# Half-wise waits and another order behind the last tile in a merged attention and mixture stage

## The chip, the cores and the metric

The kernel runs on one core of a Trainium2 chip. The time is the device time of one execution in microseconds (us), as a median of several runs. Its engines are TensorE (PE; its weight loads are shown apart as PEld), VectorE (DVE), ScalarE (ACT), GpSimd (POOL) and SyncE (SP, which here only starts DMAs).

## The reference, cut to what matters

The program is a network of four layers, each an attention block and a feed-forward block. The change lies in one stage of it, which does two things at once: the mixture of experts of the third layer, and the attention of the fourth (`_L3_xattn_ref`). That attention takes, for each of 16 heads, 128 queries against 128 keys, keeps the 32 largest scores of each row, takes the softmax over those and applies it to the values:

```python
def _L3_xattn_ref(query, key, value, Wq, Wk):
    NUM_HEADS = 16
    SCALE = DIM_ATTN ** (-0.5)          # DIM_ATTN = 8
    TOP_K = 32
    q = _split_heads(query @ Wq.T, b, sq)
    k = _split_heads(key @ Wk.T, b, sk)
    v = _split_heads(value, b, sk)
    scores = jnp.einsum('bhqa,bhka->bhqk', q, k) * SCALE
    top_vals = jax.lax.top_k(scores, TOP_K)[0]
    cutoff = top_vals[..., -1:]
    masked = jnp.where(scores >= cutoff, scores, -jnp.inf)
    w = jax.nn.softmax(masked, axis=-1)
    e = jnp.einsum('bhqk,bhka->bhqa', w, v)
    return e.transpose(0, 2, 1, 3).reshape(b, sq, d)
```

The result, times a gate, is added to `x` of shape (32, 128, 128).

## The kernel before

The stage is `l3_attention`. Its unit is a tile: one of the 32 batch elements, 128 rows with 16 heads. All engines run at the same time, and each goes through its own written list of steps, in order: `schedule(eng, steps)` walks a counter c and calls each `(step, behind)` of the list with tile c - behind, if that tile exists. On SP, PE and ACT, middle rounds are a hardware loop of four tiles; on POOL and DVE all are written out. Every step begins with waits on semaphores that other engines count up, so an engine that stands in a wait holds back everything behind it in its list. The mixture's steps (`hide`, `output`, `gelu`, `take_y`, `add_experts` and more) run four tiles ahead, so that the last rounds hold attention alone.

The attention of tile c goes like this:
- PE makes `scores`, ACT copies them to SBUF (`take_scores`, L2637).
- DVE finds in `cutoffs` the 32 largest of each row of each head: four rounds of MAX8 (L2754), which gives the next eight, with three MATCH_REPLACE8 (L2756) between, which strike them out. It goes through heads 0 to 7 first (half 0), then 8 to 15 (half 1). Each instruction counts `found` up, FINDS = 112 for a tile.
- POOL negates the largest of each head in `negate_max` (L2393, tile `nm`) once all 112 are counted.
- ACT takes the exponentials of score + nm in `exps` (L2625, 16 instructions, four for each part n of four heads), which wait for `nm`.
- POOL compares the scores with the 32nd largest (`above`, L2409, four instructions for a part) and multiplies the exponentials with that (L2414), in `mask`, part by part. There is one tile `above`, and each comparison waits for the multiplication before it.
- PE transposes the masked probabilities of a part (`turn_probs`, L2511), ACT copies them (`take_p`, L2606, tile `pT`), PE multiplies them with the values (`apply`, L2521). The four parts follow each other.
- DVE divides by the sums (`divide`, L2763 and L2765, tile `o_norm`), POOL adds that to `x` (`add_attention`, L2420).

`exps` and `mask` of a tile run one round behind its `cutoffs`, the transposes, copies and `apply` two rounds behind, `divide` and `add_attention` three. In the round c = 32, the first behind the last `cutoffs` of tile 31, the lists therefore hold: for ACT, the exponentials of tile 31 and then the copies of tile 30; for POOL, `nm` and the masks of tile 31 and the addition of tile 29; for DVE, the division of tile 29.

There is one `o_norm` and one bank for the outputs of `apply`. Hence these two waits, which the diff does not touch:

```python
                def apply(q, c, n):
                    if n == 0:
                        wait(pe, o_ready, q, 1, c)      # divide(c-1) is done
                def divide(q, c):
                    wait(dve, av_mm, q, NQ, NQ * (c + 1))
                    wait(dve, x_done, q, 1, c)          # add_attention(c-1) is done
```

Of the kernel before, what the change touches and what calls it, by code (L numbers as in the profile page):

```python
# [15 lines left out]
NB = 32  # L16
# [2217 lines left out]
def l3_attention(nc, k):  # L2234
# [4 lines left out]
    H, DA, ROUNDS = 16, 8, 4  # L2239
    Q4, NQ = 4, 4  # L2240
    SC = DA ** -0.5
    BODY = 4
    LAST_LAG = 3
    AHEAD = 4
    FIRST = BODY
    LOOPS = (NB - AHEAD - FIRST) // BODY
# [6 lines left out]
    with ExitStack() as ctx:  # L2253
# [10 lines left out]
        top = [s.sb(f"top{i}", [P, ROUNDS, H, 8]) for i in two]  # L2264
        nm = [s.sb(f"nm{i}", [P, H]) for i in two]
# [24 lines left out]
        p, rest, eq = (spare(score[3], i * NE, NB, E) for i in range(3))  # L2290
# [25 lines left out]
        FINDS = (2 * ROUNDS - 1) * H  # L2316
        BASE_STEPS, NORM_STEPS = 3, 10

        def wait(eng, sem, q, per_element, value):

            n = q * int(BODY * per_element) + value
            if not isinstance(q, int) or n >= 1:
                eng.wait_ge(sem, n)

        def schedule(eng, steps, loops=LOOPS, first=-AHEAD):

            def run(q, c):
                for step, behind in steps:
                    if not isinstance(q, int) or 0 <= q * BODY + c - behind < NB:
                        step(q, c - behind)  # L2330

            for c in range(first, FIRST):
                run(0, c)
            if loops:
                with eng.Fori(0, loops) as q:
                    for c in range(FIRST, FIRST + BODY):
                        run(q, c)
            for c in range(FIRST, NB + LAST_LAG - loops * BODY):
                run(loops, c)
# [13 lines left out]
        def in_group(step, at):  # L2353

            return lambda q, u: step(q, u // GT) if u % GT == at else None
# [4 lines left out]
        def for_part(step, n):  # L2360

            return lambda q, c: step(q, c, n)

        with nc.Block() as block:
# [17 lines left out]
            def _(pool):  # L2382
# [4 lines left out]
                    pool.memset(t[:, :, :], 1.0).then_inc(filled, 1)  # L2387
                pool.wait_ge(filled, 4)

                def negate_max(q, c):  # L2390
                    wait(pool, found, q, FINDS, FINDS * (c + 1))
                    wait(pool, probs_done, q, H, H * (c - 1))
                    pool.tensor_scalar(nm[c % 2][:, :], top[c % 2][:, 0, :, 0:1].rearrange("p h o -> p (h o)"), -1.0,  # L2393
                                       None, ALU.mult).then_inc(nm_ready, 1)

                def take_v(q, c):
# [2 lines left out]
                    pool.tensor_scalar(v[c % 4][:, :, 0:DA], v_raw[c % 2][:, :].rearrange("p (h d) -> p h d", h=H),  # L2399
                                       k.tg[:, 3:4], None, ALU.mult).then_inc(v_ready, 1)  # L2400

                def mask(q, c):
                    for n in range(NQ):
                        hs = slice(Q4 * n, Q4 * n + Q4)
                        wait(pool, found, q, FINDS, FINDS * (c + 1))
                        wait(pool, masked, q, NQ, NQ * c + n)
                        for i in range(Q4):
                            h = Q4 * n + i
                            ins = pool.tensor_scalar(above[:, i, :], score[c % 4][:, h, :],  # L2409
                                                     top[c % 2][:, ROUNDS - 1, h, 7:8], None, ALU.is_ge)  # L2410
                        ins.then_inc(compared, 1)
                        wait(pool, compared, q, NQ, NQ * c + n + 1)
                        wait(pool, probs_done, q, H, H * c + Q4 * n + Q4)
                        pool.tensor_tensor(probs[c % 2][:, hs, :], probs[c % 2][:, hs, :], above[:, :, :], ALU.mult  # L2414
                                           ).then_inc(masked, 1)
# [39 lines left out]
                def norm_scale(q, g):  # L2455
                    n = NORM_STEPS * g

                    def done(i):
# [19 lines left out]
                    pool.tensor_tensor(rstd[:, :], spread[:, :], k.neg_half[:, 0:GT], ALU.pow).then_inc(norm_step, 1)  # L2478
                    done(9)
                    pool.tensor_tensor(shift[:, :], mean[:, :], rstd[:, :], ALU.mult).then_inc(norm_step, 1)  # L2480
                schedule(pool, [(negate_max, 1), (in_group(norm_scale, 1), 2 - AHEAD), (take_v, -1), (mask, 1),
                                (add_experts, 1 - AHEAD), (in_group(add_base, 1), -AHEAD),
                                (in_group(stage_weights, 0), -AHEAD), (add_attention, 3)], loops=0)

            @block.tensor
            def _(pe):
# [106 lines left out]
            def _(act):  # L2593
# [24 lines left out]
                    ins.then_inc(y_ready, 1)  # L2618

                def exps(q, c, n):  # L2620
                    if n == 0:
                        wait(act, nm_ready, q, 1, c + 1)
                        wait(act, p_mm, q, NQ, NQ * (c - 1))
                    for h in range(Q4 * n, Q4 * n + Q4):
                        ins = act.activation(probs[c % 2][:, h, :], score[c % 4][:, h, :], ACT.Exp,  # L2625
                                             bias=nm[c % 2][:, h:h + 1]).then_inc(probs_done, 1)
# [44 lines left out]
                for u in two:  # L2671
                    for at in range(2 * EX):
# [11 lines left out]
                               (take_queries, -1), (for_part(gelu, 4), -AHEAD), (for_part(gelu, 5), -AHEAD),  # L2684
                               (for_part(take_p, 2), 2), (for_part(take_scores, 0), -1), (for_part(gelu, 6), -AHEAD),
                               (for_part(gelu, 7), -AHEAD), (in_group(take_bias, 1), -AHEAD),
                               (for_part(take_p, 3), 2), (in_group(take_weights, 0), -AHEAD), (for_part(take_scores, 2), -1)], first=2 - AHEAD)

            @block.vector
            def _(dve):  # L2690
# [49 lines left out]
                def cutoffs(q, c, half):  # L2740
                    t = top[c % 2]
                    n = FINDS // 2 * half
                    first = H // 2 * half
                    if half == 0:
                        wait(dve, masked, q, NQ, NQ * (c - 1))
                        wait(dve, nm_ready, q, 1, c - 1)
                    wait(dve, s_ready, q, NQ, NQ * c + first // Q4 + 2)
                    for step in range(2 * ROUNDS - 1):
                        for h in range(first, first + H // 2):
# [437 lines left out]
```

## Time and profile before

| what | value |
|---|---|
| median of 3 runs | 3108.95 us (3099.05 to 3109.38) |
| the profiled execution | 3108.43 us, its span 3106.5 us |
| DVE's first MAX8 of the stage, its last | 1819.1 us, 2638.2 us |
| the stage's last addition to x | 2671.41 us |
| first work of the stage behind it | 2672.22 us |
| busy over the span | PE 92%, PEld 73%, DVE 65%, ACT 59%, POOL 46% |

Times in the trace count from the span's start. An engine's row says when it started, for how long it ran, and in brackets how long the engine stood idle ahead of it and whose instruction ended that. Several instructions of a kind in a row are merged (x16), and their time is that of all together. PEclk is the clock that TensorE was granted, 1.00 for 2.4 GHz and 0.50 for 1.2 GHz.

### The profile page before, as it was taken

Reading aid. Unit: us, or ns where it says so; the run is one execution under the profiler, and the core shown is the slowest. Engines: PE = TensorE matmul, PEld = TensorE weight load, DVE = VectorE, ACT = ScalarE, POOL = GpSimd, SP = SyncE. Lnnn points to the kernel's source line nnn. Section 1 sums busy time; section 2 is a strip of 40 time slices with the busy share of each in tenths; the row PEclk is TensorE's granted clock in tenths of the full one; section 3 lists DMA queues with packets and bytes.
Section 4 is the critical chain, followed back from the end, with each engine's and each line's share of the span. In section 5 each row is a group of like instructions: output and inputs, shape, how many; then the busy total and the mean of one; then the engine's idle time right before and its main releaser. Section 6 shows DMA issues by size and latency. Waiting matters only on the chain. (4 is left out here: it accounts for less than half of the span.)

```text
span 3106.5 us, 70161 instructions
## 1 busy us (share of the span) xinstructions
PE 2845.7 (92%) x21784; PEld 2260.2 (73%) x21784; DVE 2029.1 (65%) x7986; ACT 1824.0 (59%) x5314; POOL 1430.8 (46%) x1723
## 2 busy tenths in 40 slices
PE   7999969987997989999999899999999995597999
PEld 5888854434775778888888777888888874486676
DVE  4544536764653456666666459999999999486433
ACT  5777734443553356666666567888888873353333
POOL 2122117762542434444444248888887876552000
PEclk9999979987998999999999998999999985597999
DMA  3000023433763311111111000000000000001000
GB/s 114 6 5 6 5 64 74 82 82 112 262 233 94 126 49 54 54 54 54 54 54 54 16 11 13 14 13 13 13 13 13 13 14 32 2 18 36 7 10 11
DMA packets 99460, 151.82 MB, mean 49 GB/s; under 512 B 11312, under 2 KB 39488, under 8 KB 98752
## 3 DMA queue, kind: packets, MB, share of 16 engines
q1 hardware_dynamic: 99296, 149.96, 16.1%
q8 instruction: 63, 1.03, 0.1%
q14 instruction: 101, 0.83, 0.1%
HBM read 103.33 MB, written 46.47 MB: 48 GB/s over the span
## 5 line engine op out<-in xcount | busy, mean ns | idle before, releaser
L1899 POOL TENSOR_TENSOR l2a_probs<-l2a_probs,l2a_inv 128x1024 f32<-128x1024 f32 x128 | 242.5, 1895 | 369.3 <-DVE l2a_inv L2065 369.2
L2010 ACT ACTIVATE l2a_probs<-l2a_s_ps,l2a_nm 128x256 f32<-128x256 f32 x512 | 236.8, 474 | 199.1 <-DVE l2a_nm L2041 199.1
L2754 DVE MAX8 l3a_top<-l3a_work 128x8 f32<-128x128 f32 x1536 | 327.4, 347 | 0.0
L2540 PEld LDWEIGHTS l3a_l2o_ps<-net_arena 128*128 128x128 f32 x2016 | 278.7, 224 | 40.4 <-issue 36.9
L2409 POOL TENSOR_SCALAR l3a_above<-l3a_score,l3a_top 128x128 f32<-128x128 f32 x512 | 300.1, 603 | 16.4 <-POOL l3a_probs L2414 7.7
L2540 PE MATMUL l3a_l2o_ps<-net_arena 128*128 128x128 f32 x2016 | 285.2, 309 | 11.5 <-ACT net_l1f_gate L2616 11.5
L2756 DVE MATCH_REPLACE8 l3a_work<-l3a_top,l3a_work 128x128 f32<-128x128 f32 x1024 | 277.6, 346 | 0.0
L2528 PE MATMUL l3a_l2h_ps<-net_cols,net_arena 128*128 (+1 forms) x1024 | 251.1, 388 | 11.2 <-ACT net_arena L2647 9.2
L2528 PEld LDWEIGHTS l3a_l2h_ps<-net_cols,net_arena 128*128 128x128 f32 x1024 | 185.0, 191 | 64.0 <-ACT net_arena L2647 22.7
L721 ACT ACTIVATE l0a_probs<-l0a_score_ps,l0a_nm 128x128 f32<-128x128 f32 x512 | 180.2, 382 | 73.4 <-DVE l0a_nm L770 73.4
L2647 ACT ACTIVATE net_arena<-l3a_l2h_ps,net_l2f_b 128x256 f32<-128x256 f32 x512 | 210.5, 493 | 16.3 <-PE l3a_l2h_ps L2528 13.7
L2521 PEld LDWEIGHTS l3a_o_ps<-l3a_v,l3a_pT 128*128 128x128 f32 x1024 | 147.8, 216 | 76.7 <-ACT l3a_pT L2606 67.2
L755 POOL TENSOR_TENSOR l0a_v<-l0a_v,l0a_inv 128x1024 f32<-128x1024 f32 x32 | 60.9, 1903 | 300.5 <-DVE l0a_inv L794 300.5
L2521 PE MATMUL l3a_o_ps<-l3a_v,l3a_pT 128*128 128x9 f32 x1024 | 147.5, 272 | 52.7 <-ACT l3a_pT L2606 52.7
L2041 DVE TENSOR_REDUCE l2a_nm<-l2a_s_ps 128x2 f32<-128x512 f32 x256 | 159.0, 684 | 28.3 <-PE l2a_s_ps L1922 28.2
L2414 POOL TENSOR_TENSOR l3a_probs<-l3a_probs,l3a_above 128x512 f32<-128x512 f32 x128 | 163.0, 1274 | 31.3 <-ACT l3a_probs L2625 21.7
L2625 ACT ACTIVATE l3a_probs<-l3a_score,l3a_nm 128x128 f32<-128x128 f32 x512 | 156.8, 398 | 23.1 <-POOL l3a_nm L2393 22.8
L770 DVE TENSOR_REDUCE l0a_nm<-l0a_score_ps 128x4 f32<-128x512 f32 x128 | 82.2, 684 | 124.8 <-PE l0a_score_ps L681 124.8
L2224 DVE SCALAR_TENSOR_TENSOR net_x<-l3f_o_ps,net_weight,net_x 128x128 f32 (+1 forms) x256 | 72.1, 345 | 139.9 <-PE l3f_o_ps L2141 139.5
L2176 ACT ACTIVATE l3f_hidden<-l3f_h_ps 128x512 f32<-128x512 f32 x128 | 76.4, 598 | 145.6 <-PE l3f_h_ps L2132 145.5
L1973 PE MATMUL l2a_side_ps<-net_ident,l2a_probs 128*128 128x128 f32 x1024 | 153.4, 279 | 1.0 <-POOL l2a_probs L1899 0.7
L2756 DVE MATCH_VALUE_LOAD l3a_work<-l3a_top,l3a_work 128x8 f32 x1024 | 150.3, 150 | 0.0
(520 smaller groups left out, 7268.8 us busy)
## 6 DMA issues: line engine op xcount, KB each, us to landing
kv_ahead<-l1a_kept SPq DMA_DIRECT2D x128, 256.0 KB, 2.6
l0f_code<-code_rows SPq DMA_DIRECT2D x32, 512.0 KB, 10.7
l2a_kT<-kv_ahead SPq DMA_DIRECT2D x64, 256.0 KB, 2.6
l2a_v<-kv_ahead SPq DMA_DIRECT2D x64, 256.0 KB, 2.6
l1a_shift<-neg_top SPq DMA_DIRECT2D x16, 512.0 KB, 4.8
l1f_chosen<-mask_code SPq DMA_DIRECT2D x64, 128.0 KB, 3.2
keys_ahead<-l1f_keys_kept SPq DMA_DIRECT2D x32, 256.0 KB, 3.2
l3a_kT<-keys_ahead SPq DMA_DIRECT2D x32, 256.0 KB, 2.6
```

The costliest lines, as they stand in the source:

```text
L721: act.activation(probs[c % 2][:, h, :], score[g][:, i * P:(i + 1) * P], ACT.Exp, bias=nm[:, h:h + 1], accum_out=sums[c % 2][:, h:h + 1]).t ...
L1899: pool.tensor_tensor(p[:, :, :], p[:, :, :], per_row(inv[c % 2][a][:, :, :].rearrange("p i o -> p (i o)"), KV), ALU.mult).then_inc(scaled, 1)
L2010: act.activation(probs[c % 2][a][:, 2 * i + odd, :], s_ps[a][odd][:, i * KV:(i + 1) * KV], ACT.Exp, bias=nm[c % 2][a][:, i, odd:odd + 1], ...
L2041: dve.tensor_reduce(nm[c % 2][a][:, :, odd:odd + 1].rearrange("p i o -> p (i o)"), s_ps[a][odd][:, :].rearrange("p (i s) -> p i s", i=2), ...
L2409: ins = pool.tensor_scalar(above[:, i, :], score[c % 4][:, h, :], top[c % 2][:, ROUNDS - 1, h, 7:8], None, ALU.is_ge)
L2414: pool.tensor_tensor(probs[c % 2][:, hs, :], probs[c % 2][:, hs, :], above[:, :, :], ALU.mult).then_inc(masked, 1)
L2521: ins = pe.matmul(o_ps[:, h, :], pT[n % 2][:, i, :], v[c % 4][:, h, :], start=True, stop=True)
L2528: ins = pe.matmul(h_ps[i][:, n * WIDE:(n + 1) * WIDE], w1[:, expert(u, x), 2 * i + n, :], k.cols[:, ds(group(q, u) * WIDE, WIDE)], start=T ...
L2540: ins = pe.matmul(output_bank(u, x)[:, at:at + D], hidden[2 * x + n][:, i, j * P:(j + 1) * P], w2[:, expert(u, 2 * x + n), i, :], start=(i ...
L2647: ins = act.activation(hidden[x][:, 2 * i + n, :], h_ps[i][:, n * WIDE:(n + 1) * WIDE], ACT.Gelu, bias=b1[:, e, 2 * i + n:2 * i + n + 1])
L2754: ins = dve.max(t[:, step // 2, h, :], src)
L2756: ins = dve.match_replace(work[:, h, :], t[:, step // 2, h, :], src, LOWEST)
```

## The change

It has two parts. First, `negate_max` and `mask` on POOL are split in halves of eight heads: half 0 waits for the first 56 of the 112 finds alone. `exps` waits for the first half of `nm` ahead of part 0, and for the second ahead of part 2. In the running stage both halves of `negate_max` stand one behind the other, and so do both of `mask`.

Second, `schedule` takes another list, `draining`, for the rounds c = 32 and up. On POOL it interleaves the halves: `nm`, mask, `nm`, mask. On ACT it puts the four copies of the tile two back ahead of the sixteen exponentials of the tile one back.

```diff
-        def schedule(eng, steps, loops=LOOPS, first=-AHEAD):
+        def schedule(eng, steps, loops=LOOPS, first=-AHEAD, draining=None):
 
             def run(q, c):
-                for step, behind in steps:
+                drain = draining and isinstance(q, int) and q * BODY + c >= NB
+                for step, behind in draining if drain else steps:
...
-                def negate_max(q, c):
-                    wait(pool, found, q, FINDS, FINDS * (c + 1))
+                def negate_max(q, c, half):
+                    hs = slice(H // 2 * half, H // 2 * (half + 1))
+                    wait(pool, found, q, FINDS, FINDS * c + FINDS // 2 * (half + 1))
                     wait(pool, probs_done, q, H, H * (c - 1))
-                    pool.tensor_scalar(nm[c % 2][:, :], top[c % 2][:, 0, :, 0:1].rearrange("p h o -> p (h o)"), -1.0,
+                    pool.tensor_scalar(nm[c % 2][:, hs], top[c % 2][:, 0, hs, 0:1].rearrange("p h o -> p (h o)"), -1.0,
                                        None, ALU.mult).then_inc(nm_ready, 1)
...
-                def mask(q, c):
-                    for n in range(NQ):
+                def mask(q, c, half):
+                    for n in range(NQ // 2 * half, NQ // 2 * (half + 1)):
                         hs = slice(Q4 * n, Q4 * n + Q4)
-                        wait(pool, found, q, FINDS, FINDS * (c + 1))
+                        wait(pool, found, q, FINDS, FINDS * c + FINDS // 2 * (half + 1))
...
-                schedule(pool, [(negate_max, 1), (in_group(norm_scale, 1), 2 - AHEAD), (take_v, -1), (mask, 1),
+                schedule(pool, [(for_part(negate_max, 0), 1), (for_part(negate_max, 1), 1), (in_group(norm_scale, 1), 2 - AHEAD),
+                                (take_v, -1), (for_part(mask, 0), 1), (for_part(mask, 1), 1),
                                 (add_experts, 1 - AHEAD), (in_group(add_base, 1), -AHEAD),
-                                (in_group(stage_weights, 0), -AHEAD), (add_attention, 3)], loops=0)
+                                (in_group(stage_weights, 0), -AHEAD), (add_attention, 3)], loops=0,
+                         draining=[(for_part(negate_max, 0), 1), (for_part(mask, 0), 1), (for_part(negate_max, 1), 1),
+                                   (for_part(mask, 1), 1), (add_attention, 3)])
...
                 def exps(q, c, n):
+                    if n % 2 == 0:
+                        wait(act, nm_ready, q, 2, 2 * c + n // 2 + 1)
                     if n == 0:
-                        wait(act, nm_ready, q, 1, c + 1)
                         wait(act, p_mm, q, NQ, NQ * (c - 1))
...
+                         draining=[*((for_part(take_p, n), 2) for n in range(NQ)), *((for_part(exps, n), 1) for n in range(NQ))])
...
-                        wait(dve, nm_ready, q, 1, c - 1)
+                        wait(dve, nm_ready, q, 2, 2 * (c - 1))
```

How the instructions stand on ACT behind the last scores, before: the exponentials of tile 30 (x16), the copies of tile 29 (x4), the exponentials of tile 31 (x16), then the copies of tiles 30 and 31 (x8).

```order
L2637 ACTIVATE l3a_score<-l3a_s_ps 128x512 x2
L2625 ACTIVATE l3a_probs<-l3a_score,l3a_nm 128x128 x16
L2606 ACTIVATE l3a_pT<-l3a_p_ps 128x512 x4
L2625 ACTIVATE l3a_probs<-l3a_score,l3a_nm 128x128 x16
L2606 ACTIVATE l3a_pT<-l3a_p_ps 128x512 x8
```

And with the change (its line numbers are some lines higher):

```order
L2643 ACTIVATE l3a_score<-l3a_s_ps 128x512 x2
L2631 ACTIVATE l3a_probs<-l3a_score,l3a_nm 128x128 x16
L2611 ACTIVATE l3a_pT<-l3a_p_ps 128x512 x8
L2631 ACTIVATE l3a_probs<-l3a_score,l3a_nm 128x128 x16
L2611 ACTIVATE l3a_pT<-l3a_p_ps 128x512 x4
```

The four copies of tile 30 moved from behind the exponentials of tile 31 to ahead of them.

On POOL, in the same place, with buffer numbers (tile 31 has `nm1`, `probs1`, `score3`), before:

```order
L2420 TENSOR_TENSOR net_x<-net_x,l3a_o_norm 128x128
L2393 TENSOR_SCALAR l3a_nm1<-l3a_top1 128x16
L2409 TENSOR_SCALAR l3a_above<-l3a_score3,l3a_top1 128x128 x4
L2414 TENSOR_TENSOR l3a_probs1<-l3a_probs1,l3a_above 128x512
L2409 TENSOR_SCALAR l3a_above<-l3a_score3,l3a_top1 128x128 x4
L2414 TENSOR_TENSOR l3a_probs1<-l3a_probs1,l3a_above 128x512
L2409 TENSOR_SCALAR l3a_above<-l3a_score3,l3a_top1 128x128 x4
L2414 TENSOR_TENSOR l3a_probs1<-l3a_probs1,l3a_above 128x512
L2409 TENSOR_SCALAR l3a_above<-l3a_score3,l3a_top1 128x128 x4
L2414 TENSOR_TENSOR l3a_probs1<-l3a_probs1,l3a_above 128x512
L2420 TENSOR_TENSOR net_x<-net_x,l3a_o_norm 128x128 x3
```

With the change:

```order
L2422 TENSOR_TENSOR net_x<-net_x,l3a_o_norm 128x128
L2395 TENSOR_SCALAR l3a_nm1<-l3a_top1 128x8
L2411 TENSOR_SCALAR l3a_above<-l3a_score3,l3a_top1 128x128 x4
L2416 TENSOR_TENSOR l3a_probs1<-l3a_probs1,l3a_above 128x512
L2411 TENSOR_SCALAR l3a_above<-l3a_score3,l3a_top1 128x128 x4
L2416 TENSOR_TENSOR l3a_probs1<-l3a_probs1,l3a_above 128x512
L2395 TENSOR_SCALAR l3a_nm1<-l3a_top1 128x8
L2411 TENSOR_SCALAR l3a_above<-l3a_score3,l3a_top1 128x128 x4
L2416 TENSOR_TENSOR l3a_probs1<-l3a_probs1,l3a_above 128x512
L2411 TENSOR_SCALAR l3a_above<-l3a_score3,l3a_top1 128x128 x4
L2416 TENSOR_TENSOR l3a_probs1<-l3a_probs1,l3a_above 128x512
L2422 TENSOR_TENSOR net_x<-net_x,l3a_o_norm 128x128 x3
```

The second half of `nm` moved behind the second multiplication; the additions of tiles 29, 30 and 31 (x3) still stand last. In every earlier round the one `nm` of 16 columns became two of 8, directly behind each other. PE, DVE and SP have the same instructions in the same order.

## Rows read from the trace of the kernel before

**Rows 1.** The busy time by stretches; columns: stretch, its us, busy us of each engine, PEclk, DMA share, GB/s.
```profile
2400.00:2500.00 100.00, 96.23 (x620) 83.03 (x618) 99.86 (x637) 82.26 (x210) 81.11 (x133) 0.93 0.05 14
...
2640.00:2680.00 40.00, 21.62 (x92) 18.71 (x92) 8.71 (x47) 8.42 (x21) 18.04 (x24) 0.50 0.00 1
```

**Rows 2.** What DVE waited for, 1815 to 2640: us in total, times, longest.
```profile
DVE l3a_top L2754 <- ACT l3a_score L2637: 18.2, 1, 18.2
DVE l3a_inv L2763 <- PE l3a_o_ps L2521: 2.1, 3, 0.9
```

**Rows 3.** What POOL and ACT waited for, 1850 to 2600, the two waits around nm.
```profile
POOL l3a_nm L2393 <- DVE l3a_top L2754: 72.6, 27, 6.4
...
ACT l3a_probs L2625 <- POOL l3a_nm L2393: 6.2, 2, 5.2
```

**Rows 4.** Timeline, 2600 to 2631: start, us, engine, line, what, idle before.
```profile
2600.59 1.69 DVE L2754 MAX8 l3a_top<-l3a_score 128x8 f32<-128x128 f32 x8
...
2603.97 0.45 POOL L2420 TENSOR_TENSOR net_x<-net_x,l3a_o_norm 128x128 f32<-128x128 f32 x1
...
2609.28 1.09 ACT L2637 ACTIVATE l3a_score<-l3a_s_ps 128x512 f32<-128x512 f32 x2 [4.02 <-PE l3a_s_ps L2504]
...
2613.27 0.27 POOL L2393 TENSOR_SCALAR l3a_nm<-l3a_top 128x16 f32<-128x16 f32 x1 [8.85 <-DVE l3a_top L2754]
...
2613.58 1.63 DVE L2754 MAX8 l3a_top<-l3a_score 128x8 f32<-128x128 f32 x8
2613.58 4.80 ACT L2625 ACTIVATE l3a_probs<-l3a_score,l3a_nm 128x128 f32<-128x128 f32 x16 [3.21 <-POOL l3a_nm L2393]
...
2630.95 0.90 PEld L2511 LDWEIGHTS l3a_p_ps<-net_ident,l3a_probs 128*128 128x128 f32 x4
```

**Rows 5.** Timeline, 2636 to 2659, the drain.
```profile
2636.82 1.74 DVE L2754 MAX8 l3a_top<-l3a_work 128x8 f32<-128x128 f32 x8
2638.36 0.35 DVE L2763 RECIPROCAL l3a_inv<-l3a_o_ps 128x16 f32<-128x16 f32 x1
2638.65 0.27 POOL L2393 TENSOR_SCALAR l3a_nm<-l3a_top 128x16 f32<-128x16 f32 x1 [9.42 <-DVE l3a_top L2754]
2638.75 0.29 DVE L2765 TENSOR_TENSOR l3a_o_norm<-l3a_o_ps,l3a_inv 128x128 f32<-128x128 f32 x1
2638.89 2.35 POOL L2409 TENSOR_SCALAR l3a_above<-l3a_score,l3a_top 128x128 f32<-128x128 f32 x4
2638.96 4.80 ACT L2625 ACTIVATE l3a_probs<-l3a_score,l3a_nm 128x128 f32<-128x128 f32 x16 [9.57 <-POOL l3a_nm L2393]
2641.32 1.27 POOL L2414 TENSOR_TENSOR l3a_probs<-l3a_probs,l3a_above 128x512 f32<-128x512 f32 x1
...
2644.29 1.78 PEld L2521 LDWEIGHTS l3a_o_ps<-l3a_v,l3a_pT 128*128 128x128 f32 x8 [12.44 <-ACT l3a_pT L2606]
...
2645.81 0.90 PEld L2511 LDWEIGHTS l3a_p_ps<-net_ident,l3a_probs 128*128 128x128 f32 x4
...
2647.15 0.60 ACT L2606 ACTIVATE l3a_pT<-l3a_p_ps 128x512 f32<-128x512 f32 x1 [2.91 <-PE l3a_p_ps L2511]
2647.80 1.78 PEld L2521 LDWEIGHTS l3a_o_ps<-l3a_v,l3a_pT 128*128 128x128 f32 x8 [1.09 <-ACT l3a_pT L2606]
...
2654.14 0.45 POOL L2420 TENSOR_TENSOR net_x<-net_x,l3a_o_norm 128x128 f32<-128x128 f32 x1
...
2656.72 0.26 DVE L2763 RECIPROCAL l3a_inv<-l3a_o_ps 128x16 f32<-128x16 f32 x1 [17.69 <-PE l3a_o_ps L2521]
2657.02 0.29 DVE L2765 TENSOR_TENSOR l3a_o_norm<-l3a_o_ps,l3a_inv 128x128 f32<-128x128 f32 x1
...
2658.32 1.78 PEld L2521 LDWEIGHTS l3a_o_ps<-l3a_v,l3a_pT 128*128 128x128 f32 x8 [1.09 <-ACT l3a_pT L2606]
```

**Rows 6.** Instructions that use nm, 2500 to 2700: ns min/median/max.
```profile
L2625 ACT ACTIVATE l3a_probs<-l3a_score,l3a_nm x96: 386/389/417, 2513.7 to 2643.4; 128x128 f32<-128x128 f32 x96
```

More of the change, by code:

```diff
@@ L2686, in _ @@
                                (for_part(gelu, 7), -AHEAD), (in_group(take_bias, 1), -AHEAD),
-                               (for_part(take_p, 3), 2), (in_group(take_weights, 0), -AHEAD), (for_part(take_scores, 2), -1)], first=2 - AHEAD)
+                               (for_part(take_p, 3), 2), (in_group(take_weights, 0), -AHEAD), (for_part(take_scores, 2), -1)], first=2 - AHEAD,
+                         draining=[*((for_part(take_p, n), 2) for n in range(NQ)), *((for_part(exps, n), 1) for n in range(NQ))])
             @block.vector
```

## The prediction, made before the changed kernel was run

> **What bounds the kernel now.** Four views, in this order. First the busy time by stretches [rows 1]: from 2400 to 2500 us, a stretch inside the merged stage, DVE is busy 99.86 us of 100, PE 96.23, ACT 82.26, POOL 81.11. Behind the last tile (2640 to 2680) no engine is busy for more than 22 of 40 us and PEclk is 0.50, which is the 1.2 GHz level. Second, what DVE waits for over the whole stage [rows 2]: 18.2 us once, for the first scores, and 2.1 us in three waits of `divide`. So DVE, with `cutoffs`, sets the pace of 32 tiles of some 25.5 us, and nothing that only makes POOL or ACT start earlier can shorten it by more than about 2 us. Third, what POOL and ACT wait for in the running stage [rows 3]: POOL stands 72.6 us in 27 waits, 2.7 us each, ahead of `negate_max`; ACT waits for `nm` in only two of its visits, 6.2 us. ACT usually comes to `exps` after `nm` is ready, so an earlier `nm` buys it nothing there. Fourth, the timeline of the last two tiles [rows 4, 5]: this is where time can move, since from DVE's last MAX8 on everything is one serial chain.
>
> Tiles are 0 to 31; (31,2) means part 2, heads 8 to 11, of tile 31.
>
> **The running stage: 0.** Removed: nothing. Added: one `negate_max` instruction per tile, 0.27 us at most [rows 4], on POOL. It runs while POOL waits for the second half of the maxima anyway (2.7 us on average [rows 3]). Queued behind the second `negate_max` are `take_v` and `mask`, whose wait is for the same find as before. ACT's new wait ahead of `exps` part 2 is for an instruction that ends when the single one did. DVE asks POOL only for the masks of the tile two back: those of tile 29 were done when POOL took the next step at 2603.97, and DVE began tile 31 at 2613.58 [rows 4], 9.6 us of cover. Bounds: -2.1 us if all waits of `divide` vanish [rows 2], +31 x 0.27 = +8.4 us if the cover were gone. I take 0, as 9.6 us of cover is far from gone.
>
> **Tile 30: ACT gains 2.35 us.** At 2609.28 + 1.09 = 2610.37 ACT is free and now stands until 2613.58, for `nm` of tile 30 [rows 4]. POOL is free at 2603.97 + 0.45 = 2604.42, and the first half's maxima are known by then: DVE began the second half of tile 30 at 2600.59. So the first 8 exponentials go into the gap. One costs (4.80 - 0.39) / 15 = 0.294 us in a row [rows 4, 6], so the rest ends 8 x 0.294 = 2.35 us earlier; it can't be more, since the second 8 still wait for DVE's last MAX8. The copies and multiplications of tile 29 shift with it, and the transposes of (30,0) start at 2630.95 - 2.35 = 2628.60.
>
> **Tile 30's copies are ahead of tile 31's exponentials now.** Before, ACT stood in `exps(31,0)` until 2638.96, and `take_p(30,0)` came only behind it, with PE's `apply(30,0)` at 2644.29 [rows 5]. After, `take_p(30,0)` can run at about 2630. But `apply(30,0)` waits for `o_ready` 30, that is for `divide(29)`, and DVE does that behind all cutoffs of tile 31: o_norm is written at 2638.75 to 2639.04 [rows 5]. So the copies stand again, behind a wait that the change leaves in place:
> - `apply(30,0)`: 2639.04 + 0.05 (the hand-off from 2647.15 + 0.60 to 2647.80) = 2639.09, 5.20 earlier than before.
> - From it to the next copy 2647.15 - 2644.29 = 2.86; from part to part 2647.80 - 2644.29 = 3.51. `take_p(30,3)`: 2639.09 + 2.86 + 2 x 3.51 = 2648.97, ending 2649.57.
> - Only then does ACT begin `exps(31,0)`, which before began at 2638.96: 10.6 later. Four exponentials are done after 3 x 0.294 + 0.39 = 1.27: 2650.84.
>
> **POOL's masks of tile 31 are held by that.** POOL has done its half of `nm` and `above` for (31,0) by about 2632; its multiplication stands for `exps(31,0)` until 2650.89, against 2641.32 before: +9.57. Queued behind it on POOL: the rest of mask half 0, the second half of `nm` (done before only if POOL were free; it is not, so it comes at about 2656, though its maxima are there at 2638.4), mask half 1 and `add_attention(29)`. From the first multiplication to that addition took 2654.14 - 2641.32 = 12.82; the inserted `nm` costs 0.24 (2638.65 to 2638.89) but fills the 0.2 us in which POOL waited between two parts, net +0.03. `exps(31,2)` behind the second `nm` takes 1.27 and is ready before its multiplication. `add_attention(29)`: 2650.89 + 12.85 = 2663.74.
>
> **Who waits for the addition.** `divide(30)` needs o_norm free (`x_done` 30), so `add_attention(29)`; `apply(31,0)` needs `divide(30)`. Before, both came in time: the reciprocal at 2656.72 followed PE. After: 2663.74 + 0.45 + 0.05 = 2664.24 reciprocal, + 0.30 + 0.29 for o_norm, + 0.05: `apply(31,0)` at 2664.88 against 2658.32 [rows 5]: **+6.56 us**. The copy (31,0) is ready by about 2659 and doesn't set it. The rest, four parts of 3.51 us and the last division, is the same and moves as a whole, and so does all that follows the stage.
>
> **Sum.** 0 + 6.56. The profiled execution took 3108.43 (span 3106.5), so 3115.0; it is 0.5 under the median of 3108.95, so the median comes to 3115.5. Ten hand-offs of 0.05 to 0.1 us and the early parts add about +-1.5 us.
>
> **A rule that speaks against the change.** DVE's eight MAX8 took 1.63 us while POOL ran `above` beside them (2613.58) and 1.74 us with POOL idle (2636.82) [rows 4, 5], so POOL's company costs DVE nothing here. The change puts `above` of (31,0), 2.35 us, beside the cutoffs of tile 31. The Trainium skill, "SBUF — State Buffer", section "SBUF: two separate sides", says that GpSimd and a VectorE instruction with two SBUF inputs or in a 2-port mode exclude one another for the whole instruction. If that held here, DVE's end and so `apply(30,0)` would be 2.35 us later.
>
> **Rivals.**
> - *The copies run free* (the wait for `divide(29)` doesn't bind). Then the copies of tile 30 follow the transposes at 2628.60 by 1.34 (2645.81 to 2647.15) and end at 2628.60 + 1.34 + 3 x 3.51 + 0.60 = 2641.07; multiplication at 2642.39, addition 2655.24, `apply(31,0)` 1.14 later, 2656.38: -1.9 us, 3107.0. It is what one expects who counts ACT's order alone. The code's wait speaks against it. Chance 0.06.
> - *PE's clock rises in the drain.* At 2.4 GHz PE's share of a 3.51 us part, 2.91, would halve at best, so up to 1.45 us less for each of 3 parts ahead of and 4 behind POOL's chain: -10.2, 3105.3. Against it: PEclk is 0.50 from 2640 to 2680, and 0.93 in the running stage [rows 1], and the change puts a longer pause of PE into it. "TensorE: Matmul & The Clock Gate" in the Trainium skill ("What's actually happening") says that activity releases the throttle. Chance 0.05.
> - *DVE is blocked by POOL's earlier `above`*: 3115.5 + 2.35 = 3117.8, chance 0.03.
> - *Slower by over 0.5%: the stage's pace breaks.* If POOL's masks became the last to release DVE, each of 31 tiles would pay the added instruction, 0.27 + 0.05: +9.9, with the drain +16.5: 3125.4. It decides once POOL ends mask c-2 later than DVE ends tile c-1, that is once 9.6 us of cover are used up. Chance 0.03.
> - *The drain order isn't what the text says*, or a wait is misread: no change, 3109. Chance 0.05.
>
> **How the numbers follow.** Forecast 0.78. A measurement of this kernel can tell about 0.5% (15.5 us) from no change; from 2638.4 to the end of the drain (2658.32 and four parts of 3.51) are some 34 us, and no case moves half of it downward. Of three runs before, one was 10 us lower (3099.05); if the median falls on such a run the forecast reads 3105.5. The range of 3105 to 3119 holds the forecast with this, the two rivals at 3107.0 and 3105.3, no change and the blocked DVE; left out are the broken pace and combinations. Faster 0.02, same 0.94, slower 0.04.
>
> **What would show it.** Right: DVE's last MAX8 unmoved; ACT's last four `take_p` of tile 30 with some 12 us from the first to the second, ended by PE; `exps(31,0)` at about 2649.5; POOL idle from about 2632 to 2651 for ACT; `nm` (31, second half) near 2656; the last but one reciprocal released by POOL's addition, not by PE; the last one, and all behind it, about 6.5 us later. Wrong: copies of tile 30 3.5 us apart throughout (the first rival), weight loads of 0.19 us in the drain (the second), or DVE waits between 1850 and 2600 us.

## The result, and the profile after

The changed kernel takes 3116.12 us (median of 9 runs, 3105.55 to 3119.70), the kernel before 3103.91 us beside it (9 runs, 3099.05 to 3109.38): ratio 1.0026, 95% interval 1.0016 to 1.0036, that is +8.1 us (+5.0 to +11.2); the plain difference of the two medians is 12.2. So it is slower: the interval leaves out 1, though the difference is smaller than the 0.5% (15.5 us) that the prediction took as the least that can be told from no change. The profiled execution took 3113.95 us (span 3112.2), against 3108.43 (span 3106.5) before.

The running stage looks as before. Here are the busy times by stretches, in the columns of [rows 1], of which it answers the first two, and what DVE waited for over the stage, which answers [rows 2]:

```profile
2400.00:2500.00 100.00, 96.31 (x620) 83.16 (x620) 99.86 (x640) 82.19 (x210) 81.79 (x138) 0.93 0.05 14
2620.00:2640.00 20.00, 9.30 (x42) 8.12 (x42) 17.97 (x114) 1.79 (x3) 10.14 (x16) 0.50 0.00 1
2640.00:2680.00 40.00, 19.87 (x84) 16.90 (x84) 3.27 (x16) 8.83 (x23) 13.55 (x20) 0.50 0.00 1
```

```profile
DVE l3a_top L2761 <- ACT l3a_score L2643: 18.2, 1, 18.2
DVE l3a_inv L2770 <- PE l3a_o_ps L2526: 5.1, 3, 2.9
```

From 2400 to 2500 us DVE is again busy 99.86 of 100 us, and POOL's share rose by 0.7 us (81.11 to 81.79). The added instructions cost about that: four tiles pass in this stretch, each with two `nm` of 0.24 us in place of one of 0.27. DVE's three waits for PE are 5.1 us now against 2.1.

The drain is where the two traces part. The timeline of after from the last tile's maxima to the last addition, to be laid beside [rows 5] (columns: start, us, engine, line, what, idle before it and who ended it):

```profile
2627.51 0.90 PEld L2516 LDWEIGHTS l3a_p_ps<-net_ident,l3a_probs 128*128 128x128 f32 x4
...
2628.32 2.33 POOL L2411 TENSOR_SCALAR l3a_above<-l3a_score,l3a_top 128x128 f32<-128x128 f32 x4
...
2628.62 1.64 DVE L2761 MAX8 l3a_top<-l3a_work 128x8 f32<-128x128 f32 x8
2628.86 0.60 ACT L2611 ACTIVATE l3a_pT<-l3a_p_ps 128x512 f32<-128x512 f32 x1 [2.91 <-PE l3a_p_ps L2516]
...
2635.88 1.64 DVE L2761 MAX8 l3a_top<-l3a_work 128x8 f32<-128x128 f32 x8
...
2638.15 1.84 PE L2526 MATMUL l3a_o_ps<-l3a_v,l3a_pT 128*128 128x9 f32 x8 [9.33 <-DVE l3a_o_norm L2772]
...
2640.97 0.60 ACT L2611 ACTIVATE l3a_pT<-l3a_p_ps 128x512 f32<-128x512 f32 x1 [11.52 <-PE l3a_p_ps L2516]
...
2647.99 0.60 ACT L2611 ACTIVATE l3a_pT<-l3a_p_ps 128x512 f32<-128x512 f32 x1 [2.91 <-PE l3a_p_ps L2516]
2648.48 2.43 ACT L2631 ACTIVATE l3a_probs<-l3a_score,l3a_nm 128x128 f32<-128x128 f32 x8
...
2649.89 1.26 POOL L2416 TENSOR_TENSOR l3a_probs<-l3a_probs,l3a_above 128x512 f32<-128x512 f32 x1 [19.25 <-ACT l3a_probs L2631]
...
2654.97 0.24 POOL L2395 TENSOR_SCALAR l3a_nm<-l3a_top 128x8 f32<-128x8 f32 x1
...
2655.25 2.44 ACT L2631 ACTIVATE l3a_probs<-l3a_score,l3a_nm 128x128 f32<-128x128 f32 x8 [4.34 <-POOL l3a_nm L2395]
2657.60 0.57 ACT L2611 ACTIVATE l3a_pT<-l3a_p_ps 128x512 f32<-128x512 f32 x1
...
2662.68 0.45 POOL L2422 TENSOR_TENSOR net_x<-net_x,l3a_o_norm 128x128 f32<-128x128 f32 x1
2663.23 0.26 DVE L2770 RECIPROCAL l3a_inv<-l3a_o_ps 128x16 f32<-128x16 f32 x1 [25.23 <-POOL net_x L2422]
...
2663.93 1.78 PEld L2526 LDWEIGHTS l3a_o_ps<-l3a_v,l3a_pT 128*128 128x128 f32 x8 [12.01 <-issue]
...
2677.03 0.45 POOL L2422 TENSOR_TENSOR net_x<-net_x,l3a_o_norm 128x128 f32<-128x128 f32 x1 [12.68 <-DVE l3a_o_norm L2772]
```

Read it downward as one chain. DVE's last MAX8 comes at 2635.88. PE starts `apply(30,0)` at 2638.15, released by o_norm, that is by `divide(29)`. ACT's copy (30,0) had been done since 2629.46, so the next copy stands 11.52 us for PE. Behind the fourth copy (2647.99) ACT begins the exponentials of tile 31, at 2648.48; POOL has stood 19.25 us for them. POOL's addition of tile 29 begins at 2662.68, and DVE's reciprocal for tile 30 (2663.23) was released by that addition, where in [rows 5] it was PE that released it.

To split the difference I cut each execution at three instructions: the first MAX8 of the stage, the start of its last eight MAX8, and the start of the last addition to x. S is from the first to the second (the running stage), D from the second to the third (the drain). What follows is 434.2 to 435.4 us in all nine kernels. Each S and D is read from the one profiled execution of its kernel.

| | first MAX8 | S | D | rest | span |
|---|---|---|---|---|---|
| before | 1819.1 | 817.7 | 34.59 | 435.1 | 3106.5 |
| after | 1815.4 | 820.5 | 41.15 | 435.2 | 3112.2 |
| difference | -3.7 | +2.8 | +6.56 | +0.1 | +5.7 |

What the change does to the drain is +6.56. The first MAX8 comes between 1813.0 and 1820.4 us in the nine profiles, though none of the edits touches what lies ahead of it, so -3.7 is within what executions differ by. S needs the experiments.

### The profile page after: what moved, and what is told of

It reads as the page before. It is cut to its first block and busy times, and to the rows that moved or that the text cites. A ratio compares the mean times of both kernels' runs of the same rounds, so it can differ in the third digit from the quotient of the medians.

```text
span 3112.2 us, 70259 instructions
## 1 busy us (share of the span) xinstructions
PE 2850.5 (92%) x21784; PEld 2260.4 (73%) x21784; DVE 2027.4 (65%) x7986; ACT 1820.0 (58%) x5314; POOL 1434.3 (46%) x1755
## 5 line engine op out<-in xcount | busy, mean ns | idle before, releaser
L2761 DVE MAX8 l3a_top<-l3a_work 128x8 f32<-128x128 f32 x1536 | 314.1, 276 | 0.0
L2763 DVE MATCH_REPLACE8 l3a_work<-l3a_top,l3a_work 128x128 f32<-128x128 f32 x1024 | 268.9, 275 | 0.0
L2141 PEld LDWEIGHTS l3f_o_ps<-net_arena,l3f_hidden 128*128 128x128 f32 x1024 | 124.2, 192 | 29.7 <-issue 18.2
```

What stands on the lines that cost most here:

```text
L2141: ins = pe.matmul(o_ps[u % OB][:, j * D:(j + 1) * D], hidden[u % 2][:, i, j * P:(j + 1) * P], w2[:, u % E, i, :], start=(i == 0), stop=(i ...
L2761: ins = dve.max(t[:, step // 2, h, :], src)
L2763: ins = dve.match_replace(work[:, h, :], t[:, step // 2, h, :], src, LOWEST)
```

## Experiments: one half of the change at a time

**The halves alone.** The changed kernel without its drain lists, so that ACT and POOL keep the running order behind the last tile:

```diff
-                                (in_group(stage_weights, 0), -AHEAD), (add_attention, 3)], loops=0,
-                         draining=[(for_part(negate_max, 0), 1), (for_part(mask, 0), 1), (for_part(negate_max, 1), 1),
-                                   (for_part(mask, 1), 1), (add_attention, 3)])
+                                (in_group(stage_weights, 0), -AHEAD), (add_attention, 3)], loops=0)
...
-                         draining=[*((for_part(take_p, n), 2) for n in range(NQ)), *((for_part(exps, n), 1) for n in range(NQ))])
```

> The change's first part alone: the waits by halves of eight heads; no other order behind the last tile. Two measures are read from the trace: S, from the stage's first MAX8 to the start of its last eight (817.7 us before, 820.5 with the whole change), and D, from there to the start of the last addition to x (34.6 before, 41.15 with the whole change). My theory (the order of ACT's list costs the drain, the halves gain 2.35 us of exponentials there, the running stage is untouched): D 32.2, S 817.7 +-1, the time 2.4 us under before. Rival A (the halves slow the running stage): S about 820.5, so the time is within 1 us of before. Rival B (the second half of nm, taken late, is what costs the drain): D 34.6 or less as well, since here POOL takes both halves of nm one behind the other; this run doesn't speak against B, the next does.

Measured: 0.9992 of before (0.9981 to 1.0003), S 818.05, D 32.09. The drain is 2.50 us shorter than before. The timeline, in the columns above, shows from where:

```profile
2631.05 1.64 DVE L2758 MAX8 l3a_top<-l3a_work 128x8 f32<-128x128 f32 x8
...
2633.04 2.44 ACT L2629 ACTIVATE l3a_probs<-l3a_score,l3a_nm 128x128 f32<-128x128 f32 x8 [7.08 <-POOL l3a_nm L2395]
2635.39 0.57 ACT L2609 ACTIVATE l3a_pT<-l3a_p_ps 128x512 f32<-128x512 f32 x1
...
2636.01 1.78 PEld L2524 LDWEIGHTS l3a_o_ps<-l3a_v,l3a_pT 128*128 128x128 f32 x8 [12.44 <-ACT l3a_pT L2609]
...
2663.14 0.45 POOL L2422 TENSOR_TENSOR net_x<-net_x,l3a_o_norm 128x128 f32<-128x128 f32 x1 [13.29 <-DVE l3a_o_norm L2769]
```

ACT does only eight exponentials (2.44 us) behind the last maxima, the other eight of tile 31 being done already, and copy (30,0) follows at 2635.39. `apply(30,0)` starts 4.96 us behind the start of the last MAX8 (2636.01 less 2631.05), where it was 7.47 in [rows 5] (2644.29 less 2636.82). So the halves by themselves help the drain, by about the term of 2.35 us that the prediction had given to tile 30 alone. The time alone would not show it: its interval holds 1. S is 818.05, like before: the halves do not slow the running stage. In this run, too, the reciprocal of tile 30 (2648.74) was released by POOL's addition (2648.18), and yet nothing was lost by it: `apply(31,0)` at 2650.05 followed its copy, some 0.7 us after the division would have let it start. A reciprocal that waits for the addition is a loss only where `apply` then waits for the division.

**The new order on ACT alone.** The kernel before, with whole tiles of maxima and exponentials, and only ACT's drain list (with the lines of `schedule` that read it, shown in the change above):

```diff
-                               (for_part(take_p, 3), 2), (in_group(take_weights, 0), -AHEAD), (for_part(take_scores, 2), -1)], first=2 - AHEAD)
+                               (for_part(take_p, 3), 2), (in_group(take_weights, 0), -AHEAD), (for_part(take_scores, 2), -1)], first=2 - AHEAD,
+                         draining=[*((for_part(take_p, n), 2) for n in range(NQ)), *((for_part(exps, n), 1) for n in range(NQ))])
```

> The kernel before with one edit: behind the last tile ACT copies the probabilities of tile 30 ahead of the exponentials of tile 31. No halves, POOL as before. My theory: exps(31,0) begins only behind take_p(30,3), which hangs on divide(29): D 41.1 (+6.5), S 817.7 +-1, the time 6.5 us above before. Rival B (the halves and POOL's late second nm make the drain long): D 34.6, or shorter. Rival A: S 817.7 here, since the halves are not in.

Measured: 1.0015 (1.0004 to 1.0025), S 820.4, D 41.17.

```profile
2637.86 1.64 DVE L2756 MAX8 l3a_top<-l3a_work 128x8 f32<-128x128 f32 x8
...
2642.95 0.60 ACT L2607 ACTIVATE l3a_pT<-l3a_p_ps 128x512 f32<-128x512 f32 x1 [9.15 <-PE l3a_p_ps L2512]
...
2650.46 4.77 ACT L2626 ACTIVATE l3a_probs<-l3a_score,l3a_nm 128x128 f32<-128x128 f32 x16
...
2651.87 1.27 POOL L2415 TENSOR_TENSOR l3a_probs<-l3a_probs,l3a_above 128x512 f32<-128x512 f32 x1 [9.69 <-ACT l3a_probs L2626]
...
2679.03 0.45 POOL L2421 TENSOR_TENSOR net_x<-net_x,l3a_o_norm 128x128 f32<-128x128 f32 x1 [12.68 <-DVE l3a_o_norm L2767]
```

The pattern of after is all there without a single half: a copy that waited 9.15 us for PE, the exponentials behind the fourth copy, POOL idle 9.69 us for them, D within 0.02 us of after's. So the order on ACT makes the loss, and it swallows what the halves win. And S is 820.4 in a kernel whose running stage is that of before, word for word, and where 817.7 +-1 had been expected; its DVE waits ahead of `divide` are 4.8 us. The longer S of after is therefore no effect of the halves. Over all nine profiled executions S is 820.4 to 820.8 where those waits sum to 4.8 to 5.3 us (after, this one, the third experiment), and 817.7 to 818.7 where they sum to 2.1 to 2.9 us (the rest; in the sixth and seventh a wait in the drain is left out, and the three kernels with the early `divide(29)` have its 0.5 us in S). What makes an execution the one or the other stays open.

## Experiments: which wait makes the loss

**The addition ahead of the masks.** The changed kernel; POOL does `add_attention(29)` before it turns to tile 31's masks, so that `divide(30)` has its buffer early:

```diff
-         draining=[(for_part(negate_max, 0), 1), (for_part(mask, 0), 1), (for_part(negate_max, 1), 1),
-                   (for_part(mask, 1), 1), (add_attention, 3)])
+         draining=[(for_part(negate_max, 0), 1), (add_attention, 3), (for_part(mask, 0), 1),
+                   (for_part(negate_max, 1), 1), (for_part(mask, 1), 1)])
```

> The changed kernel with one step moved on POOL behind the last tile: add_attention(29) ahead of the first half of the masks of tile 31, instead of behind the second. D is, as before, the time from the start of the stage's last eight MAX8 to the start of its last addition (34.6 before, 41.15 with the change). My theory: with the change apply(31,0) waits for divide(30), which waits for that addition; moved ahead, the wait is gone and what is late next is the copy (31,0) behind exps(31,3): apply(31,0) 5.7 us earlier than in the change, D 35.5. Rival C: that addition isn't what holds apply(31,0), but the copies or the masks themselves: D 41.

Measured: 0.9995 (0.9981 to 1.0008), D 35.45, 5.70 less than after's.

```profile
2643.14 0.45 POOL L2422 TENSOR_TENSOR net_x<-net_x,l3a_o_norm 128x128 f32<-128x128 f32 x1 [9.76 <-DVE l3a_o_norm L2772]
...
2654.96 1.26 POOL L2416 TENSOR_TENSOR l3a_probs<-l3a_probs,l3a_above 128x512 f32<-128x512 f32 x1 [9.04 <-ACT l3a_probs L2631]
2655.61 0.26 DVE L2770 RECIPROCAL l3a_inv<-l3a_o_ps 128x16 f32<-128x16 f32 x1 [12.55 <-PE l3a_o_ps L2526]
...
2660.31 2.44 ACT L2631 ACTIVATE l3a_probs<-l3a_score,l3a_nm 128x128 f32<-128x128 f32 x8 [4.34 <-POOL l3a_nm L2395]
2662.66 0.57 ACT L2611 ACTIVATE l3a_pT<-l3a_p_ps 128x512 f32<-128x512 f32 x1
...
2676.39 0.45 POOL L2422 TENSOR_TENSOR net_x<-net_x,l3a_o_norm 128x128 f32<-128x128 f32 x1 [8.18 <-DVE l3a_o_norm L2772]
```

The addition now comes at 2643.14, released by o_norm, and the reciprocal of tile 30 (2655.61) is released by PE again. POOL's multiplication still stands 9.04 us for ACT. So the last link of the chain, the addition held behind the masks, carries 5.70 of the 6.56 us. The 0.86 us that remain (35.45 less 34.59) come by another way: copy (31,0), at 2662.66, stands in ACT's order behind the last eight exponentials, and these stood 4.34 us for the second `nm`, which POOL does behind its late first masks.

**`divide(29)` in time.** The changed kernel; DVE does `divide(29)` between two rounds of the last tile's second half instead of behind it:

```diff
                     for step in range(2 * ROUNDS - 1):
+                        if c == NB - 1 and half == 1 and step == 2:
+                            divide(q, NB - 3)
...
-                schedule(dve, [(divide, 3), (for_part(cutoffs, 0), 0), (for_part(cutoffs, 1), 0),
+                schedule(dve, [(lambda q, c: divide(q, c) if c != NB - 3 else None, 3), (for_part(cutoffs, 0), 0), (for_part(cutoffs, 1), 0),
```

> The changed kernel with one step moved on DVE: divide(29) behind the first two of the seven rows of finds of the last half of cutoffs, instead of behind all of them; ACT and POOL as in the change. My theory: the gap of 12 us between the first and the second copy of tile 30 closes, exps(31,0) begins 8.6 us earlier, POOL and apply(31,0) follow: D 32.0. If the gap has another cause, the copies still stand until DVE is done and D is 40.6 (the 0.5 us of divide moved ahead of the last MAX8).

Measured: 0.9982 (0.9967 to 0.9998), D 32.05, 9.10 less than after's.

```profile
2631.53 0.60 ACT L2611 ACTIVATE l3a_pT<-l3a_p_ps 128x512 f32<-128x512 f32 x1 [2.91 <-PE l3a_p_ps L2516]
...
2635.03 0.60 ACT L2611 ACTIVATE l3a_pT<-l3a_p_ps 128x512 f32<-128x512 f32 x1 [2.91 <-PE l3a_p_ps L2516]
...
2639.04 1.64 DVE L2763 MAX8 l3a_top<-l3a_work 128x8 f32<-128x128 f32 x8
...
2642.54 2.43 ACT L2631 ACTIVATE l3a_probs<-l3a_score,l3a_nm 128x128 f32<-128x128 f32 x8
...
2643.95 1.26 POOL L2416 TENSOR_TENSOR l3a_probs<-l3a_probs,l3a_above 128x512 f32<-128x512 f32 x1 [10.64 <-ACT l3a_probs L2631]
...
2657.29 0.26 DVE L2772 RECIPROCAL l3a_inv<-l3a_o_ps 128x16 f32<-128x16 f32 x1 [16.61 <-POOL net_x L2422]
```

The copies run 3.51 us apart from the first on (2631.53, 2635.03), where after had 12.1 us between these two. The last one is done 2 us behind the last maxima, and the exponentials start at 2642.54, 3.50 us behind the start of the last MAX8 (2639.04) instead of 12.60. With `divide(29)` out of its way the same order on ACT is no loss, but it gives no more than the halves give alone (D 32.09). The reciprocal of tile 30 still waits 16.61 us for POOL's addition, and `apply(31,0)`, at 2657.99, waits for that division.

## Experiments: what the drain can give

**Exponentials between the copies.** The changed kernel with ACT's list in the order copy 0, exponentials 0 to 3, copies 1 to 3; DVE and POOL as in after:

```diff
-         draining=[*((for_part(take_p, n), 2) for n in range(NQ)), *((for_part(exps, n), 1) for n in range(NQ))])
+         draining=[(for_part(take_p, 0), 2), *((for_part(exps, n), 1) for n in range(NQ)),
+                   *((for_part(take_p, n), 2) for n in range(1, NQ))])
```

> The changed kernel with another order on ACT behind the last tile: take_p(30,0), exps(31,0 to 3), take_p(30,1 to 3). My theory: ACT's wait for divide(29) is filled by the exponentials, POOL's masks and its addition of tile 29 come in time, and the chain of copies 3.51 us apart from apply(30,0), some 2.2 us behind the start of the last eight MAX8, sets the end: D 29.4, 5.2 us under before and 11.7 under the change; time 5 us under before, or 2 to 3 if rival A (S 820.5) holds. Rival B: D near 41, as POOL's list is as in the change.

Measured: 0.9969 (0.9955 to 0.9982), D 29.36.

```profile
2629.59 2.43 ACT L2631 ACTIVATE l3a_probs<-l3a_score,l3a_nm 128x128 f32<-128x128 f32 x8
...
2638.13 2.44 ACT L2631 ACTIVATE l3a_probs<-l3a_score,l3a_nm 128x128 f32<-128x128 f32 x8 [6.10 <-POOL l3a_nm L2395]
...
2641.22 0.60 ACT L2611 ACTIVATE l3a_pT<-l3a_p_ps 128x512 f32<-128x512 f32 x1 [0.64 <-PE l3a_p_ps L2516]
...
2665.48 0.45 POOL L2422 TENSOR_TENSOR net_x<-net_x,l3a_o_norm 128x128 f32<-128x128 f32 x1 [13.57 <-DVE l3a_o_norm L2773]
```

Only copy (30,0) can be done ahead of `apply(30,0)`, since PE's list has the transposes of (30,1) behind it, so only that one is. ACT fills the 11.52 us in which it stood for PE with all sixteen exponentials (2629.59 and 2638.13) and then stands only 0.64 us for PE ahead of copy (30,1). The eight parts of the two tiles follow one another without a break: 2.24 us from the last MAX8 to the first `apply`, seven pitches of 3.51, and 2.55 for the last part, its division and the addition make 29.36.

**Both together.** The early `divide(29)` of the fourth experiment, ACT's list as copy 0, exponentials 0 and 1, copies 1 to 3, exponentials 2 and 3, and POOL's addition between the two mask halves. Of the edit, ACT's list:

```diff
-         draining=[*((for_part(take_p, n), 2) for n in range(NQ)), *((for_part(exps, n), 1) for n in range(NQ))])
+         draining=[(for_part(take_p, 0), 2), (for_part(exps, 0), 1), (for_part(exps, 1), 1),
+                   *((for_part(take_p, n), 2) for n in range(1, NQ)), (for_part(exps, 2), 1), (for_part(exps, 3), 1)])
```

> A version meant to beat both: as the run before, and besides divide(29) is done by DVE in the midst of the last tile's second half of cutoffs (behind the first two of its seven rows of finds), add_attention(29) stands on POOL between the two halves of the last masks, and ACT's order is take_p(30,0), exps(31,0), exps(31,1), take_p(30,1 to 3), exps(31,2), exps(31,3). My theory: apply(30,0) no longer waits for DVE, the copies of tiles 30 and 31 are 3.51 us apart throughout, D 20.2, 14.4 us under before; the time 13.9 us under before (-0.45%), less 2 to 3 us if rival A holds. If something else than divide(29) held the chain, D stays near 29.

Measured: 0.9949 (0.9937 to 0.9962), D 20.26: median 3090.79 us, faster than both kernels.

```profile
2625.64 0.60 ACT L2611 ACTIVATE l3a_pT<-l3a_p_ps 128x512 f32<-128x512 f32 x1 [2.91 <-PE l3a_p_ps L2516]
...
2626.14 2.44 ACT L2631 ACTIVATE l3a_probs<-l3a_score,l3a_nm 128x128 f32<-128x128 f32 x8
...
2629.15 0.60 ACT L2611 ACTIVATE l3a_pT<-l3a_p_ps 128x512 f32<-128x512 f32 x1 [0.58 <-PE l3a_p_ps L2516]
...
2653.42 0.45 POOL L2422 TENSOR_TENSOR net_x<-net_x,l3a_o_norm 128x128 f32<-128x128 f32 x1 [9.79 <-DVE l3a_o_norm L2775]
```

Exponentials fit into the gap of one pitch between two copies: 2625.64 to 2629.15 is 3.51 us, with 2.44 us of exponentials in it. PE's eight parts start 3.51 us apart from 2626.29 to 2650.84, seven of these pitches, so the serial loop of one part is now the whole drain. The three edits stand together here, and no run has two of them without the third. That POOL's addition had to move is read from the trace: `apply(31,0)` started at 2640.32, and POOL's last mask, behind which the addition stands in the change, began only at 2641.94.

**A second bank for the transposes.** In that loop PE's transposes wait for the copy that empties their one PSUM bank. The kernel above, with the odd parts turned into a bank that the expert work no longer needs (`h_ps[0]`, `l3a_l2h_ps` in the trace), and PE turning one part ahead. `turn_two(n)` is `turn_probs` with two banks; ACT's copies read the same bank. Of the edit, what PE does:

```diff
-                    wait(pe, p_ready, q, NQ, NQ * c + n)
+                    wait(pe, p_ready, q, NQ, NQ * c + n + 1 - banks)
+                    bank = h_ps[0] if banks == 2 and n % 2 else p_ps
...
+         draining=[(turn_two(0), 2), (turn_two(1), 2), (for_part(apply, 0), 2), (turn_two(2), 2),
+                   (for_part(apply, 1), 2), (turn_two(3), 2), (for_part(apply, 2), 2), (for_part(apply, 3), 2)])
```

> The best version so far (divide early, interleaved; D 20.26) with two PSUM banks for the transposed probabilities behind the last tile, and PE's list there with each transpose one part ahead of its apply. Asked: what paces the chain of 3.51 us a part, of which PE's two steps fill 2.9 and ACT's copy 0.6. If PE and copy overlap now, a part takes 2.6 to 2.9 us; the last mask of tile 31 then ends about 10 us behind the start of the last eight MAX8 and the rest takes 4.6: D 15 +-0.7, 5 us under the version without it. If TensorE's clock rises (PEclk 0.50 in the drain so far), D can't get much under 14.6 for that mask, but weight loads would read 0.19 us and not 0.33. If the pitch stays 3.51: D 20.3.

Measured: 0.9920 (0.9907 to 0.9932), D 14.56: median 3085.58 us beside 3109.51 of before, the fastest of all. Two views: the timeline, and the busy time by stretches in the columns of [rows 1].

```profile
2626.58 1.78 PEld L2527 LDWEIGHTS l3a_o_ps<-l3a_v,l3a_pT 128*128 128x128 f32 x8 [0.23 <-ACT l3a_pT L2621]
...
2629.39 1.78 PEld L2527 LDWEIGHTS l3a_o_ps<-l3a_v,l3a_pT 128*128 128x128 f32 x8 [0.39 <-ACT l3a_pT L2621]
...
2635.18 0.24 POOL L2395 TENSOR_SCALAR l3a_nm<-l3a_top 128x8 f32<-128x8 f32 x1 [1.79 <-DVE l3a_top L2777]
...
2641.66 1.26 POOL L2416 TENSOR_TENSOR l3a_probs<-l3a_probs,l3a_above 128x512 f32<-128x512 f32 x1
...
2642.97 0.72 PEld L2517 LDWEIGHTS l3a_l2h_ps<-net_ident,l3a_probs 128*128 128x128 f32 x4 [0.31 <-POOL l3a_probs L2416]
...
2648.01 0.45 POOL L2422 TENSOR_TENSOR net_x<-net_x,l3a_o_norm 128x128 f32<-128x128 f32 x1 [4.67 <-DVE l3a_o_norm L2788]
```

```profile
2620.00:2630.00 10.00, 9.31 (x42) 8.28 (x43) 9.97 (x64) 4.57 (x12) 9.46 (x15) 0.50 0.01 2
2630.00:2640.00 10.00, 8.79 (x42) 8.39 (x43) 5.63 (x34) 4.04 (x12) 7.87 (x13) 0.50 0.00 0
```

From the first `apply` to the next it is 2.81 us (2626.58 to 2629.39) in place of 3.51, and PE is busy 93% and 88% of the two stretches of 10 us. So the loop of one part no longer paces the drain. And the end is not set by PE. The second half of `nm`, at 2635.18, ended a wait of POOL for DVE's last maxima; from there POOL's comparisons and multiplications follow one another up to 2642.92 (2641.66 and 1.26), and the transposes of the last part, at 2642.97, ended a wait for POOL. D is therefore 9.47 us from the start of DVE's last MAX8 (2633.45) to the end of the last mask, and 5.09 for what is left: transposes, copy, the last two parts of `apply`, division (the expectation had about 10 and 4.6). What bounds this drain is the masks that can only begin behind the last maxima.

The measured time is some 24 us under before, more than the drain gives. Of the 23.9 us between the two profiles (spans 3106.5 and 3082.6) D is 20.03; 4.3 lie ahead of the stage (first MAX8 at 1814.8), where the edits change nothing.

## Why the prediction was right, point by point

- **The running stage: 0.** POOL's share rose by no more than its added instructions, and DVE stayed at 99.86 of 100 us. The profile had +2.8 us here and -3.7 us ahead of the stage, which the change doesn't touch; the first two experiments show the +2.8 without the halves and the halves without it. As far as one profile of each can tell, 0 holds.
- **Tile 30 gains 2.35 us.** The transposes of (30,0) start 8.37 us ahead of the start of the last MAX8 (2627.51, 2635.88), before 5.87 ahead (2630.95, 2636.82): 2.50 gained, slightly more than the 2.35 that the prediction called the most. In after it is spent in the wait for `divide(29)`. The halves alone gave 2.50 us in the drain, but there by the last tile: ACT's sixteen exponentials behind the last maxima became eight. The prediction had the size and did not say that the last tile would give the same again in another order.
- **The copies stand behind `divide(29)`.** Forecast: 12.1 us between the first and second copy. Measured: 2628.86 to 2640.97, 12.1. `apply(30,0)` was forecast 2.27 behind the start of the last MAX8 (2639.09 less 2636.82) and came 2.27 behind it (2638.15 less 2635.88).
- **Exponentials 10.6 us later.** From the last MAX8 they were at 2.14 in [rows 5]; now at 12.60 (2648.48 less 2635.88), 10.46 later. Forecast of the multiplication +9.57: it was 4.50 behind the last MAX8 and is 14.01, +9.51.
- **The second half of `nm` is late.** Forecast 2656 with the last MAX8 at 2636.82, so 19.2 behind it; measured 2654.97 less 2635.88, 19.1.
- **The addition holds `divide(30)`.** The reciprocal is released by POOL's addition after 25.23 us. `apply(31,0)`: 21.50 behind the last MAX8 before (2658.32 less 2636.82), 28.05 now (2663.93 less 2635.88): +6.55, forecast +6.56. The fourth and third experiment confirm the two waits in it one by one (-9.10 without the first, -5.70 without the second; they overlap).
- **The sum.** The profiled execution was 3113.95 against a forecast of 3115.0, since what lies outside the drain came to -1.0: +2.8, -3.7, +0.1 in the span and -0.2 around it (1.75 us against 1.93). The median of 3116.12 is 0.6 from 3115.5. Part of that is luck: the median of before beside it was 3103.91 and not 3108.95, so the measured difference of 8.1 us (12.2 between the medians) is larger than 6.56, which still lies in its interval.
- **The rivals.** *The copies run free:* refuted in after. The fourth experiment shows the free copies once `divide(29)` is early: D 2.54 us under before, of which 0.5 is the division moved into S, so 2.0 in all, where this rival said 1.9. *PE's clock rises:* PEclk stays 0.50 from 2620 to 2680. *DVE is blocked by POOL's earlier `above`:* the eight MAX8 at 2628.62 ran beside four `above` (2628.32, 2.33 us) and took 1.64 us, those at 2635.88 with POOL idle 1.64 too. So nothing was blocked in this pair. The rule of the Trainium skill that the prediction weighed ("SBUF — State Buffer", "SBUF: two separate sides") speaks of VectorE instructions with two SBUF inputs or in a 2-port mode; the rows show one input for MAX8 (`l3a_work`), and so this pair does not test the rule for the instructions that it names. *The pace breaks:* behind the first scores DVE's waits in the stage are 5.1 us in all, against 9.9 us that this rival needs; all are for PE and none for POOL's masks, and 4.8 us of such waits appear in the second experiment without the halves.

## What to carry to other kernels

A step moved ahead in an engine's in-order list helps only if what it waits for is also ahead: follow that wait from engine to engine until it ends at work that is done by then. Here three of the four copies that were put ahead of the exponentials could not run, as they hung on a `divide` that another engine did last, while the exponentials behind them could. The one bank of `apply` and the one `o_norm` then passed the delay on. In a drain, place the steps so that each fills the gap of the one before it (one copy, eight exponentials, one copy), then look at the buffers that make the remaining loop serial. And read each trace again for what ends it: behind the second bank it was no longer PE's loop but POOL's masks.

## What the runs showed that I had not expected

**The clock stayed at its lower level while PE was busy.** In the last experiment PE was busy 9.31 and 8.79 of 10 us, with PEclk 0.50, the 1.2 GHz level, in both stretches, while the running stage has 0.93 at 96% busy [rows 1]. The Trainium skill ("TensorE: Matmul & The Clock Gate", "What's actually happening") says that activity releases the throttle; in these two stretches the trace does not show it. It does later in the same run: from 2680 to 2690 us PE is busy 10.00 of 10 us with PEclk 0.77, from 2690 to 2700 it is busy 9.98 with 1.00, and it executes 243 matmuls there, against 42 in each of the two stretches of the drain. No run tells which difference between the stretches decides.

**The scatter goes with the granted clock.** Over the 24 runs of before that stand beside the first experiments, time follows the mean granted clock of the execution: 3111.65 us at 0.922, 3095.66 us at 0.929, by a fitted line 2.1 us for each 0.001. In after, 3119.70 us at 0.920 and 3105.55 us at 0.927. What makes an execution's clock higher was not tried, and a kernel that leaves out stretches at 0.50 raises its own mean, so the mean clocks of different kernels are not compared here. One run of each kernel compared would measure this scatter of some 16 us before a drain of 6.56, and that is why each profile is cut into S and D above.
